# Each weighted sum of four heads issued as one run of 16 matmuls instead of two runs of 8 a slot apart

## What is computed

```python
x = _ln(src) * (1.0 + scale) + shift
q = (x @ Wq + bq)...; k = (x @ Wk + bk)...; v = (x @ Wv + bv)...
scores = einsum('bhqd,bhkd->bhqk', q / sqrt(HEAD_DIM), k) + attention_bias
scores = where(src_mask, -inf, scores)
probs = softmax(scores, axis=-1)
ctx = einsum('bhqk,bhkd->bhqd', probs, v)        # the weighted sums
x = x + (ctx @ Wo + bo)
h = _ln(x) * g2 + beta2
ff = _gelu2(h @ W1 + b1) @ W2 + b2
return x + ff
```

## Time and profile before

| | |
|---|---|
| median of three runs | 1038.18 us |
| the profiled execution, whole | 1038.9 us |
| its span, first to last instruction | 1037.1 us |
| granted TensorE clock, mean | 0.969 of full |
| PE busy | 925.7 us, 89% |
| DVE, ACT, POOL busy | 724.2, 700.8, 684.9 us |
| the L771 matmuls | 2048 records, 137.7 us busy |
| bytes moved | 207.4 MB, 200 GB/s |

### The profile page before, as it was taken

The page is one execution under the profiler, slowest core; times in us unless marked ns, Lnnn a source line. Parts: engine busy times, 40 slices in busy tenths (PEclk is TensorE's granted clock), DMA queues, the critical chain, the costliest instruction groups (busy, mean ns, idle before and its releaser), DMA issues.

```text
span 1037.1 us, 20949 instructions
## 1 busy us (share of the span) xinstructions
PE 925.7 (89%) x6621; PEld 659.1 (64%) x6621; DVE 724.2 (70%) x1927; ACT 700.8 (68%) x1659; POOL 684.9 (66%) x391
## 2 busy tenths in 40 slices
PE   3667879999989999999989999999989999999887
PEld 1434545676667676676667776676667766676655
DVE  6846676778677776878677786878667787775541
ACT  2226778777687777777777777777777777776541
POOL 2338875977667865877667775877677775873600
PEclk8667999999999999999999999999999999999998
DMA  5399769766786669667796669766785659854200
GB/s 160 103 272 298 246 194 260 231 201 207 218 257 194 201 194 261 205 195 216 207 263 199 197 193 262 221 183 205 211 250 186 197 175 255 239 178 152 92 11 11
DMA packets 147950, 207.42 MB, mean 200 GB/s; under 512 B 14385, under 2 KB 62322, under 8 KB 147842
## 3 DMA queue, kind: packets, MB, share of 16 engines
q1 hardware_dynamic: 147842, 206.09, 67.0%
HBM read 185.05 MB, written 20.99 MB: 199 GB/s over the span
## 4 chain that ended last, share of the span: by engine, by line
PE 66%; issue 11%; ACT 9%; DVE 8%; POOL 4%; DMA 1%; DVEq 0%; SPq 0%; POOLq 0%; ACTq 0%
PE tp L812 17%; PE pv L771 9%; PE lc L717 9%; PE sc L805 9%; PE la L734 7%; PE lb L581 4%; POOL bias_s L489 3%; PE lb L751 3%; ACT pT L957 3%; PE lb L597 2%; ACT bias_s L951 2%; DVE bias_s L1337 2%; DVE la L1088 1%; PE lc L715 1%; DVE pT L1344 1%
## 5 line engine op out<-in xcount | busy, mean ns | idle before, releaser
L489 POOL TENSOR_TENSOR bias_s<-mask_f,bias_s 128x1024 f32<-128x1024 f32 x256 | 603.1, 2373 | 197.2 <-DMA bias_s<-in_bias 196.7
L951 ACT ACTIVATE bias_s<-bias_s,mx 128x512 f32<-128x512 f32 x512 | 369.9, 723 | 265.4 <-DVE mx L1337 262.9
L1337 DVE CUSTOM_DVE_ANT_0 bias_s<-sc,bias_s 128x512 f32<-128x512 f32 x512 | 346.4, 683 | 207.7 <-PE sc L805 192.8
L812 PE MATMUL tp<-ident,bias_s 128*128 128x128 f32 x2048 | 314.1, 277 | 56.9 <-ACT pT L957 53.0
L812 PEld LDWEIGHTS tp<-ident,bias_s 128*128 128x128 f32 x2048 | 247.6, 142 | 161.9 <-ACT bias_s L951 60.8
L805 PE MATMUL sc<-stk,stq 128*128 128x512 bf16 x512 | 197.1, 385 | 12.3 <-DVE mx L1337 10.2
L957 ACT COPY pT<-tp 128x512 f32<-128x512 f32 x320 | 182.5, 571 | 0.0
L771 PE MATMUL pv<-pT,v_all 128*32 128x256 f32 x2048 | 137.7, 387 | 0.6 <-issue 0.6
L1344 DVE COPY pT<-tp 128x512 f32<-128x512 f32 x192 | 131.5, 685 | 3.9 <-PE tp L812 3.9
L734 PE MATMUL la<-w_s,act_s 128*128 128x256 f32 x512 | 128.3, 380 | 1.0 <-DVE act_s L1296 1.0
L717 PE MATMUL lc<-hT,w_s 128*128 128x256 f32 x464 | 121.1, 384 | 0.0
(11 more groups left out here) (188 smaller groups left out, 844.3 us busy)
## 6 DMA issues: line engine op xcount, KB each, us to landing
bias_s<-in_bias SPq DMA_DIRECT2D x256, 512.0 KB, 4.2
stq<-q_parts SPq DMA_DIRECT2D x128, 96.0 KB, 3.7
stk<-k_parts SPq DMA_DIRECT2D x128, 96.0 KB, 4.0
k_parts<-kb SPq DMA_DIRECT2D x32, 192.0 KB, 2.3
q_parts<-qb SPq DMA_DIRECT2D x32, 192.0 KB, 2.6
xT<-in_x_t SPq DMA_DIRECT2D x8, 512.0 KB, 5.9
k_parts<-kb SPq DMA_DIRECT2D x32, 128.0 KB, 2.2
stq<-q_parts SPq DMA_DIRECT2D x64, 64.0 KB, 3.7
```

The costliest lines, as they stand in the source:

```text
L489: pool.tensor_tensor(tile, mask_f[:, :, :], tile, ALU.subtract).then_inc(s["masked"], 1)
L812: last = pe.transpose(tp[n % 2][:, kt * P:(kt + 1) * P], bias_s[:, n // 2 % NB, n % 2, kt * P:(kt + 1) * P], ident[:, :])
L951: act.activation(tile, tile, ACT.Exp, bias=mx[:, t:t + 1], scale=-1.0, accum_out=sums[:, j, head_of(hh):head_of(hh) + 1]).then_inc(s["prob ...
L1337: dve.tensor_tensor_reduce(out=tile, in0=sc[t % 2][:, :], in1=tile, scale=1.0, scalar=BIG, op0=ALU.add, op1=ALU.min, accum_out=mx[:, t:t + ...
```

## The change

`weigh` loses its argument `half`; it waits once, issues the 16 matmuls of all four key blocks, and raises `pv_done`. In `PE_AT` the two places of each group become one: 14.0 and 15.0 become 14.6, 22.0 and 23.0 become 22.6, 30.0 and 31.0 become 30.6, and 6.0 and 7.0 (for the group of the iteration before) become 6.6. No matmul is added or removed; no other engine's program changes.

```diff
 PE_AT = dict(up=0.3, q=(1.0, 2.0), v=(10.0, 11.0), xt1=12.6, k=(15.3, 16.0), down=(24.3, 25.3),
-             pv=((14.0, 15.0), (22.0, 23.0), (30.0, 31.0), (6.0, 7.0)), spread=(23.3, 7.3))
+             pv=(14.6, 22.6, 30.6, 6.6), spread=(23.3, 7.3))
...
-                def weigh(g, half):
+                def weigh(g):
                     gi = NG * i + g - (NG if g == NG - 1 else 0)
-                    if half == 0:
-                        pe.wait_ge(s["copied_v"], moved(TG * (gi + 1), False))
...
+                    pe.wait_ge(s["copied_v"], moved(TG * (gi + 1), False))
+                    pe.wait_ge(s["copied_a"], moved(TG * (gi + 1), True))
+                    pe.wait_ge(s["d_v"], 2 * (gi // NG // 2) + 2)
+                    if g % 2 == 0:
+                        wait(pe, s["d_ctx"], gi // 2)
                     v = v_all[(gi // NG // 2) % 2]
-                    for kt in range(2 * half, 2 * half + 2):
+                    for kt in range(KT):
...
-                    if half == 1:
-                        last.then_inc(s["pv_done"], 1)
+                    last.then_inc(s["pv_done"], 1)
...
-                        if (prev if g == NG - 1 else attn) and t in AT["pv"][g]:
-                            weigh(g, AT["pv"][g].index(t))
+                        if (prev if g == NG - 1 else attn) and t == AT["pv"][g]:
+                            weigh(g)
```

## The result

The changed kernel takes 1070.95 us (median of four runs, 1070.15 to 1071.73) against 1038.92 us for the kernel before in the same session: a ratio of 1.0287 over the runs, 95% interval 1.0265 to 1.0309 (the two medians by themselves are 1.031 apart). The forecast was 1054 us in a range of 1038.5 to 1066. The direction was right; the time lies above the range.

What follows compares the result with a forecast made beforehand. PE, busy 925.7 of 1037.1 us, was taken as the bound. Order +3.2 us and clock falls +13 us gave +16 us on 1038.9, 1055 us; with the runs' median 0.7 us lower, 1054 us, range 1038.5 to 1066.

Steps and rivals of the forecast that it cites:

- A joined run saves 0.23 us: Each weighted sum on PE: joining its halves saves 0.09 + 0.14 us, at most 63 x 0.23 = 14.5 us.
- Slot 6 loses its cover: Slots 6 and 7: first half moves behind `turn(2)`, which stays put; 0.86 us in each of 12 iterations, +10.3 us.
- Places 14.6, 22.6, 30.6: Joined runs at these slots save 0.23 us each, at 30.6 only every second iteration: -2.8, -2.8 and -1.5 us.
- Sum of the order: Waits and savings of the four joined places together, without the clock: 10.3 - 2.8 - 2.8 - 1.5 = +3.2 us.
- The clock falls because the half kept PE at work: Slot 6: without the half between two waits, PE's granted clock can fall; +13 us, bounds 0 and +34.
- The price of a fall: Behind slot 6: each fall of the clock costs 2.2 us, against 2.8 us lost in a stretch at the start.
- How often: Slot 6 in 12 iterations: the clock falls one time in two, bounds none and all.
- the edges: First two and last two iterations and the finish: waits of other kinds, taken at 0 with 1.5 us either way.
- The case of a fall nearly every time: Rival: the clock falls nearly every time and for longer, 12 x 2.8 + 3.2 = +37 us, 1075 us; chance 0.05.
- The whole: All iterations: +3.2 us of waits and savings and +13 us of clock, +16 us together.
- the order alone: Rival: only the exchange of order counts, clock stays at 1.00; +3.2 us, 1038 to 1046, middle 1042 us; chance 0.22.
- The one by which the saved drains decide: Rival: every saved mode change counts, `turn(2)` starts at least 0.63 us sooner; 1025 us; chance 0.09.

Runs made afterwards that it cites:

- the filled kernel: The changed kernel with the four transposes of `turn(1)` in slot 5 issued four times over: 1042.51 us, ratio 1.0012 to the kernel before.
- the kernel with slot 6 alone: The kernel before with only the group of slots 6 and 7 joined, at 6.6: 1068.19 us, ratio 1.0245; traced again, 1063.72 us, ratio 1.0228.
- the best of these kernels: The changed kernel with the group of slots 6 and 7 joined at 6.0 instead of 6.6: 1036.93 us, ratio 0.9960 to the kernel before.

## Why the prediction was right and wrong, step by step

- **A joined run saves 0.23 us.** Right: 32 records in 1.93 us, 1.87 us to the next start where the clock is full.
- **Slot 6 loses its cover.** Right in kind: `turn(2)` stayed where it was. It costs 0.7 us, not 0.86; most of the rest was taken up by a small wait of PE that was there before at `turn(6)` (369.29 in the trace of the kernel before, 0.34 us behind `score(10)` where 0.22 is usual). The prediction's "no wait on anyone up to slot 19" passed over it.
- **Places 14.6, 22.6, 30.6.** Right, 0.58 us together for 0.59 forecast, down to the wait at `turn(10)` when slot 6 sends no delay.
- **Sum of the order.** +3.2 us forecast for twelve iterations, 12 x 0.13 = 1.6 us by the filled kernel; what is missing is missing at slot 6.
- **The clock falls because the half kept PE at work.** Right, and shown three ways: work put back takes the loss away, work taken out brings it, and both together leave nothing. The new stretch, 26% busy, was called nearest to the one at 96.93 (30%); by its share it is nearer to the one at 65.60 (27%). Both had fallen, so nothing hung on it.
- **The price of a fall.** 2.2 us forecast. The eleven lengths sum to 669.3 us, those of the filled kernel to 647.5 us: 21.8 / 11 = 1.98 us.
- **How often: the step that failed.** "I take one time in two" was the mis-sized term. It was each time in the changed kernel, 12 x 1.98 = 23.8 us in place of 13, 10.6 us more, which alone carries the forecast from 1054 to 1065 us, just inside the range; the edges (below) carry it over. The one in two was a count over four stretches of the start, two of which fell. For the kernel with slot 6 alone it was nearly right (7 and 6 of 12). That where one iteration ends sets whether the next one meets a fall was not in the sum. The case of a fall nearly every time had got only 0.05, and at 1075 us it was the nearest of all; it was right in how often and too high in the price (2.8 us), which the edges made up for, so that its nearness is in part luck.
- **The edges: a second term that failed.** Taken as 0 with 1.5 us either way, without a reason from rows. They are 31.8 - 23.2 = 8.6 us, or 6.6 us when the twelfth fall, behind `turn(2)` of iteration 13 (861.60), is counted with the others as above. There are further falls at 131 and 158 us and one at 1002 us. The filled kernel, without any of these falls, still has some 3.8 us at its edges against the trace of before; what part of that is the chip's was not parted.
- **The whole.** 1.6 + 23.8 + 6.6 = 32 us against 31.8 measured between the profiled executions, where the prediction had 3.2 + 13 + 0 = 16.

Of the rivals, the order alone is what the filled kernel shows, and the changed kernel is not. The one by which the saved drains decide failed where the prediction put its point: `turn(2)` did not move. The Trainium skill, "TensorEngine Tiling (Array Packing)", Key Properties, says that a change of the tiling mode drains TensorE. The traces agree as far as a joined run saves the 0.23 us; but of the 14.5 us the best of these kernels got some 4.

## What to carry to other kernels

Work that fills a wait is free on a busy engine, and moved behind the wait it costs most of its length (0.7 of 0.86 us here); before joining two runs, look at what each of them covers. On TensorE such work can also keep the clock: here PE's two waits grew by 0.9 us (from 1.05 and 0.98 to 1.05, 0.41 and 1.50), and the fall behind them cost 2 us more, so a filler (here the same four transposes, three times more) or the joined run placed ahead of the wait is worth trying. When a fall is possible at a place that comes back each iteration, take none and all as the bounds and give "all" a real share, since the falls of one place are not independent. And a kernel whose clock falls in part of its iterations should be traced more than once before its time is believed.

## What the runs showed of the hardware

- Leaving out 8 float32 matmuls in each of 15 iterations made the kernel 1.9% slower (interval 1.5 to 2.3%); adding 12 transposes to an iteration made one 2.7% faster (1070.95 to 1042.51 us).
- The clock fell after stretches in which PE was never idle for more than 1.5 us at a time (idle 1.05, 0.41 and 1.50 us with work between).
- With equal work in the stretch the clock fell in one iteration and held in the next (1.43 of 3.98 us; and 1.02 of 3.98 us in the kernel with only slot 6 joined). Where the stretch lay against the instants at which the clock changes parted the two in every one of the 12 and the 48 iterations.
- Behind `turn(2)` a fall ended 3.4 to 7 us after it began, with PE at work throughout, and cost 1.3 to 2.8 us.
